# Two-layer attention in a vision tower: projection in f16 passes, transfers issued by ScalarE, a new order of transfers, doubled values

## What is computed

```python
def _L0_attn_ref(x, w_qkv, b_qkv, w_proj, b_proj):     # x: (64, 196, 192), normalized
    qkv = x @ w_qkv.T + b_qkv
    ...
    atten = jnp.einsum('bhqd,bhkd->bhqk', q, k) * SCALE
    atten = jax.nn.softmax(atten, axis=-1)
    out = jnp.einsum('bhqk,bhkd->bhqd', atten, v)
    out = jnp.transpose(out, (0, 2, 1, 3)).reshape(B, P, D)
    return out @ w_proj.T + b_proj
```

## Time and profile before

| | |
|---|---|
| median of three runs | 3193.28 us (3190.69 to 3194.79) |
| the profiled execution | 3213.14 us, its span 3211.4 us |
| busy in the span | PE 2835.8, DVE 2311.4, ACT 1874.4, POOL 1399.9 us |
| mean granted TensorE clock | 0.964 |

### The profile page before, as it was taken

The page is one execution under the profiler, slowest core; times in us unless marked ns, Lnnn a source line. Parts: engine busy times, 40 slices in busy tenths (PEclk is TensorE's granted clock), DMA queues, the critical chain, the costliest instruction groups (busy, mean ns, idle before and its releaser), DMA issues. The chain is left out here.

```text
span 3211.4 us, 94765 instructions
## 1 busy us (share of the span) xinstructions
PE 2835.8 (88%) x31231; PEld 2149.3 (67%) x31231; DVE 2311.4 (72%) x5442; ACT 1874.4 (58%) x3668; POOL 1399.9 (44%) x1954
## 2 busy tenths in 40 slices
PE   4999379999999999999999968898984999999997
PEld 4888245555555555555555538888864888888887
DVE  4888367777777777777777736766655777777776
ACT  3888246666666666666666637666642444444443
POOL 2777323333333344444444221565554444444444
PEclk9999579999999999999999989999987999999999
DMA  5664245556565666666666544444433433444443
GB/s 138 170 189 112 58 107 135 147 146 151 146 152 146 149 157 159 163 159 160 161 160 165 146 102 132 135 134 126 133 103 92 65 64 65 66 68 67 65 65 48
DMA packets 514471, 393.84 MB, mean 123 GB/s; under 512 B 222432, under 2 KB 487682, under 8 KB 514178
## 3 DMA queue, kind: packets, MB, share of 16 engines
q1 hardware_dynamic: 472514, 338.78, 41.4%
q0 software_dynamic: 38496, 46.38, 8.2%
q10 hardware_dynamic: 3168, 4.82, 0.6%
HBM read 232.59 MB, written 155.42 MB: 121 GB/s over the span
## 5 line engine op out<-in xcount | busy, mean ns | idle before, releaser
L657 DVE TENSOR_REDUCE a_mx<-a_mxp 98x4 f32<-98x784 f32 x768 | 746.4, 972 | 318.2 <-PE a_mxp L806 316.2
L533 ACT ACTIVATE a_pt<-a_st 98x784 f32<-98x784 f32 x768 | 632.3, 823 | 207.4 <-PE a_st L792 206.7
L1563 POOL DMA_INDIRECT out_dram<-f_yo,f_idg x202 | 330.9, 1638 | 432.5 <-DVE f_yo L1904 396.1
L479 POOL TENSOR_TENSOR a_cn<-a_ctxs,a_rec 128x392 f32<-128x392 f32 x192 | 190.0, 1019 | 531.8 <-DMA a_rec<-a_recip 531.8
L1641 ACT ACTIVATE f_hf<-f_bank,f_b1c 128x256 f32<-128x256 f32 x606 | 254.3, 473 | 236.1 <-PE f_bank L878 236.1
L821 PE MATMUL a_pv<-a_pt,a_vp 98*32 98x196 f32 x6144 | 339.0, 338 | 0.8 <-ACT a_ctxs L564 0.5
L868 PE MATMUL a_pr<-a_pf,a_cn 128*98 128x192 f32 x1536 | 332.1, 346 | 7.5 <-POOL a_cn L479 4.3
L2066 PE MATMUL f_bank<-f_w2h,f_hh 128*128 x1212 | 299.7, 247 | 25.1 <-DVE f_hl L1888 24.3
L806 PE MATMUL a_mxp<-a_kst,a_qst 48*128 48x196 f16 x3072 | 262.2, 248 | 67.1 <-DMA a_kst<-a_qk 46.5
L2067 PE MATMUL f_bank<-f_w2h,f_hl 128*128 x1212 | 298.2, 246 | 0.0
L2068 PE MATMUL f_bank<-f_w2l,f_hh 128*128 x1212 | 298.2, 246 | 0.0
(11 more groups left out here) (304 smaller groups left out, 7684.1 us busy)
## 6 DMA issues: line engine op xcount, KB each, us to landing
a_rec<-a_recip SPq DMA_DIRECT2D x256, 147.0 KB, 3.6
t_rows<-in_x_dram SPq DMA_DIRECT2D x84, 392.0 KB, 5.9
a_qst<-a_qk SPq DMA_DIRECT2D x256, 110.2 KB, 3.3
a_kst<-a_qk SPq DMA_DIRECT2D x256, 110.2 KB, 3.0
f_xg<-f_listed SPq DMA_DIRECT2D x101, 264.0 KB
a_qk<-a_qkh SPq DMA_DIRECT2D x128, 196.0 KB, 2.7
a_qk<-a_qkl SPq DMA_DIRECT2D x128, 98.0 KB, 2.9
a_qk<-a_qkh SPq DMA_DIRECT2D x128, 98.0 KB, 2.4
```

Of the source, the lines that this page charges most:

```text
L533: act.activation(pt[k % PT][:].rearrange("p j a t -> p j (a t)"), st_ps[0:half_t, :, 0:unit_t], ACT.Exp, scale=sm_scale).then_inc(exp_s, 1)
L657: dve.tensor_reduce(mx[:, a, :, 2 * p:2 * p + 2].rearrange("p q j -> p j q"), mx_ps[0:half_t, :, 0:unit_t].rearrange("p j (q t) -> p j q t ...
L1563: pool.indirect_dma_start(out, bass.IndirectOffsetOnAxis(ap=idg[i % 3][:, t:t + 1], axis=0), yo[i % 3][:, t, :], None, compute_op=ALU.add) ...
```

## The change

- The context is multiplied on POOL in one operation over all 1176 columns (`cf`), then a masked f16 half (`ch`) is made and subtracted, which leaves an f16 operand `cn` with high halves in the first 16 rows of each head's 32 and low halves in the last 16. For this the values `vp` hold each head's columns twice (second ScalarE copy, 15 columns), with the ones in the last column; the heads' columns lie 12 elements apart; and one more transfer copies context row 15 to row 31 when the sums were gathered.
- `project` is seven f16 products for each token tile (weights in a high and a low half `ph`, `pl`, and one product for the bias), two tiles into one PSUM bank, at slots 4 and 6; `out_rows` adds two tiles at once.
- `place_maxima`, the residual load and (second layer) the store of `xx` are issued by ScalarE at slots 3, 9, 8 and 0.
- SyncE's order is new, `store_parts` comes in four parts of which only the last waits for the third block of rows, and the tables of slots are new.

```diff
-        OUTS, NORM, REC = 4, 5, 64
-
-        ROWS_AT, TURN_AT, VALUES_AT = (9, 11, 6), (3, 5), (1, 2)
-        PROJECT_AT = ((2, 2, 2), (4, 4, 4), (6, 6, 6), (9, 10, 10))
-        HIGH_PART_AT, VALUES_OUT_AT = (4, 6), (1, 2)
-        LOW_PART_AT, LOW_ROWS_AT, OUT_AT = (4, 7), (9, 11, 6), (3, 4, 7, 11)
+        OUTS, NORM, REC = 2, 5, 64
+
+        ROWS_AT, TURN_AT, VALUES_AT = (9, 11, 6), (2, 3), (0, 1)
+        PROJECT_AT = (4, 4, 6, 6)
+        HIGH_PART_AT, VALUES_OUT_AT = (3, 6), (1, 2)
+        LOW_PART_AT, LOW_ROWS_AT, OUT_AT = (3, 7), (10, 11, 6), (5, 10)
         MAXIMA_AT = (2, 8)
 
-        ROWS_FIRST, PART_FIRST, CONTEXT_FIRST, VALUES_FIRST = (1, 1, 0), (0, 1), (1, 1, 1, 1, 1, 1), (0, 0)
-        NEGATED_AT, RECIP_AT, STATS_AT, AGGREGATE_AT = 6, 4, (10, 0), 2
+        ROWS_FIRST, PART_FIRST, CONTEXT_FIRST, VALUES_FIRST = (1, 1, 1), (0, 0), (0, 1, 1, 0, 0, 1), (0, 0)
+        NEGATED_AT, RECIP_AT, STATS_AT, AGGREGATE_AT = 7, 5, (9, 1), 4
...
@@ SyncE, step
                 if "M" in kinds:
                     load_stacks(s + 1, (par + 1) % 2, 1, 0)
+                if "M" in kinds:
                     load_stacks(s + 1, (par + 1) % 2, 1, 1)
                 if "P" in kinds:
                     store_parts(s + 2, par, 0)
+                    store_parts(s + 2, par, 1)
+                if "P" in kinds:
+                    store_parts(s + 2, par, 2)
...
-                if kinds.get("L") == 1:
-                    u = s + 3
-                    wait(sp, xx_s, 4 * (u - UL + 1))
-                    sp.dma_start(of_units(r_rows, u, 1), xx[:]).then_inc(res_s, 16)
-                if "C" in kinds:
-                    place_maxima(s, par, 1)
...
+                if "O" in kinds:
+                    u, b = s - 1, (par + 1) % 2
+                    waits(sp,
+                          (inv_s, u),
+                          (ctx_s, GROUPS * (u + 1)))
+                    sp.dma_start(sums[:], ctxs[b][2 * hd - 1::32].rearrange("h g (q t) -> h (g q) t", q=4)).then_inc(sum_s, 16)
+                if "O" in kinds:
+                    u, b = s - 1, (par + 1) % 2
+                    waits(sp,
+                          (cn_s, 3 * u - 2),
+                          (sum_s, 16 * (u + 1)))
+                    sp.dma_start(ctxs[b][2 * hd - 1::32], ctxs[b][hd - 1::32]).then_inc(dup_s, 16)
...
+                if "P" in kinds:
+                    load_stacks(s + 2, par, 0, 0)
+                if "P" in kinds:
+                    store_parts(s + 2, par, 3)
...
-                if "M" in kinds:
-                    place_maxima(s + 1, (par + 1) % 2, 0)
...
@@ POOL, step
                     wait(pool, pr_s, OUTS * (u - 1))
+                    wait(pool, cn_s, 3 * u)
+                    wait(pool, dup_s, 16 * (u + 1))
                     wait(pool, rec_s, REC * (u + 1))
-                    for g in range(3):
-                        pool.tensor_tensor(cn[b][:, g, :], ctxs[b][:, g, :], rec[:, g, :], ALU.mult).then_inc(cn_s, 1)
-
+                    pool.tensor_tensor(cf[:], ctxs[b][:], rec[:], ALU.mult).then_inc(cn_s, 1)
+                    pool.wait_ge(cn_s, 3 * u + 1)
+                    pool.tensor_tensor(ch[:], cf[:], low_half[:].unsqueeze(2).to_broadcast([128, 3, unit_t]), ALU.mult).then_inc(cn_s, 1)
+                    pool.wait_ge(cn_s, 3 * u + 2)
+                    pool.tensor_tensor(cn[b][:], cf[:], ch[:], ALU.subtract).then_inc(cn_s, 1)
...
@@ ScalarE, step
                     empty(k, 0)
+                    if k == 0 and kinds.get("L") == 1:
+                        u = s + 3
+                        wait(act, xx_s, 4 * (u - UL + 1))
+                        act.dma_start(of_units(r_rows, u, 1), xx[:]).then_inc(res_s, 16)
+                    if k == 3 and "C" in kinds:
+                        place_maxima(s, par, 1)
+                    if k == 8 and "O" in kinds:
+                        u, b = s - 1, (par + 1) % 2
+                        waits(act,
+                              (xo_s, OUTS * (u - 1) + 1),
+                              *(((res_s, 16 * (u - UL + 1)),) if kinds["O"] == 1 else ()))
+                        act.dma_start(xres[b][:], of_units(r_rows, u, kinds["O"])).then_inc(xres_s, 16)
+                    if k == 9 and "M" in kinds:
+                        place_maxima(s + 1, (par + 1) % 2, 0)
...
-                order = "p (x h d) -> p x h d" if layers[layer][7] else "p (x d h) -> p x h d"
-                act.copy(vp[b][:, 2 * n:2 * n + 2, :, 0:hd],
-                         misc[BANK[f"V{n}"]][0:half_t, 0:2 * dim].rearrange(order, x=2, h=heads)).then_inc(vp_s, 1)
+                order = "p (x h d) -> p x d h" if layers[layer][7] else "p (x d h) -> p x d h"
+                rows = misc[BANK[f"V{n}"]][0:half_t, 0:2 * dim].rearrange(order, x=2, h=heads)
+                pair = slice(2 * n, 2 * n + 2)
+                act.copy(vp[b][:, pair, 0:dim].rearrange("p x (d h) -> p x d h", h=heads), rows)
+                act.copy(vp[b][:, pair, dim:2 * dim - heads].rearrange("p x (d h) -> p x d h", h=heads),
+                         rows[:, :, 0:hd - 1, :]).then_inc(twice_s, 1)
...
-                wait(act, cn_s, 3 * (u - 2) + g + 1)
+                wait(act, cn_s, 3 * (u - 2) + 1)
...
@@ TensorE
-                if g6 % 3 == 0:
-                    wait(pe, vp_s, 2 * u + a + 1)
+                if g6 == 0:
+                    wait(pe, twice_s, 2 * (u + 1))
...
-                        ins = pe.matmul(pv_ps[32 * h4:32 * h4 + 32, 0:tok], vp[b][:, 2 * a + kt, h, :], pt[(first + h4) // 2 % PT][:, h4 % 2, kt, :],
+                        ins = pe.matmul(pv_ps[32 * h4:32 * h4 + 32, 0:tok], vp[b][:, 2 * a + kt, :].rearrange("p (c h) -> p c h", h=heads)[:, :, h], pt[(first + h4) // 2 % PT][:, h4 % 2, kt, :],
...
-                if x == 0:
-                    wait(pe, cn_s, 3 * u + g + 1)
-                ins = pe.matmul(pr_ps[0:half_t, 0:dim], cn[b][:, g, x * half_t:(x + 1) * half_t], pf[layer][:, g, :],
-                                start=(g == 0), stop=(g == 2))
-                if g == 2:
+                    wait(pe, cn_s, 3 * (u + 1))
+                ts, at = slice(x * half_t, (x + 1) * half_t), x % 2 * dim
+                ins = products(pe, pr_ps[0:half_t, at:at + dim],
+                               [(ones16[:], pl[layer][:, 3, :])]
+                               + [(cn[b][:, g, ts], w[layer][:, g, :]) for g in range(3) for w in (ph, pl)])
+                if x % 2 == 1:
                     ins.then_inc(pr_s, 1)
```

More of the change, by code:

```diff
@@ L109, in attention_phase @@
         wl = [sb(f"wl{i}", [128, 2, 3 * dim], F16) for i in range(NL)]
-        pf = [sb(f"pf{i}", [128, 3, dim], F32) for i in range(NL)]
+        pbias = [sb(f"pbias{i}", [rows_q, 2, 128], F32) for i in range(NL)]
+        pf = [sb(f"pf{i}", [128, 4, dim], F32) for i in range(NL)]
+        ph = [sb(f"ph{i}", [128, 4, dim], F16) for i in range(NL)]
+        pl = [sb(f"pl{i}", [128, 4, dim], F16) for i in range(NL)]
         bq = [sb(f"bq{i}", [128, QB], F32) for i in range(NL)]
@@ L191, in attention_phase @@
         sum_s = sem("sum_s")
+        dup_s = sem("dup_s")
         inv_s = sem("inv_s")
@@ L420, in _ @@
             for layer in range(NL):
-                pool.memset(praw[layer][:], 0.0).then_inc(consts, 1)
+                pool.memset(pbias[layer][:], 0.0).then_inc(consts, 1)
             pool.memset(ident[:], 0.0).then_inc(consts, 1)
@@ L569, in maxima_row, with place_maxima @@
                 act.copy(mrow[:, a, :], pv_ps[0:heads, 0:tok]).then_inc(mr_s, 1)
+            def place_maxima(u, b, a):
+                waits(act,
+                      (mr_s, 2 * u + a + 1),
+                      (ms_s[a], 32 * u))
+                for j in range(2):
+                    at = 64 * j + STACK
+                    act.dma_start(qst[b][at:at + 1, :, a, 0:tok], mrow[j::2, a, :]).then_inc(ms_s[a], 16)
             steps(step, act, between)
@@ L600, in prepare @@
                 dve.wait_ge(p_ok[layer], done + 2)
-                dve.tensor_reduce(praw[layer][:, :, :, hd + 1:hd + 2], pbv[:], AX.X, ALU.add).then_inc(p_ok[layer], 1)
+                dve.tensor_copy(praw[layer][:, :, :, hd:2 * hd], praw[layer][:, :, :, 0:hd]).then_inc(p_ok[layer], 1)
+                for part in range(2):
+                    dve.tensor_reduce(pbias[layer][:, :, 32 * part:32 * part + 1], pbv[:].rearrange("p e h d -> p e (h d)"),
+                                      AX.X, ALU.add).then_inc(p_ok[layer], 1)
                 dve.wait_ge(w_f[layer], G_READY[layer])
@@ L774, in step @@
                         for x in range(4):
-                            for g in range(3):
-                                if PROJECT_AT[x][g] == k:
-                                    project(s - 2, par, x, g, kinds["Y"])
+                            if PROJECT_AT[x] == k:
+                                project(s - 2, par, x, kinds["Y"])
                     if k == MAXIMA_AT[0] and "C" in kinds:
```

122 lines of the change are left out of this document (60 added, 62 removed).

## The result

| | before | after | forecast |
|---|---|---|---|
| time, median (us) | 3194.03 (3190.69 to 3197.79) | 3167.61 (3162.98 to 3171.36) | 3097 (3045 to 3210) |
| ratio to before, 95% interval | 1 | 0.9915 (0.9897 to 0.9933) | 0.970 |
| profiled span (us) | 3211.4 | 3169.6 | |
| one step (us) | 22.77 | 22.33 | 21.2 |

The change makes the kernel faster by 0.85%, 27 us (3194 x 0.0085), inside the range, and gives little more than a quarter of the 96 us that were forecast. The step follows from the first and last reciprocal, as in the earlier trace rows: (1866.5 - 459.8) / 63 = 22.33 us, 0.44 less, x 64 = 28 us. The two spans lie 41.8 us apart, since the profiled execution of before was itself 20 us above its median and that of after 4 us; I go by the steps and the medians.

A forecast was written before the change was run, and what follows sets the result against it. TensorE's work plus late transfers was taken as the bound. TensorE 20.6, VectorE 19.4 and POOL's loop 20.4 to 21.3 us gave a 21.2 us step; 100 us gained less 4 gave 3097 us, range 3045 to 3210.

The forecast's parts named there:

- TensorE works 21.28 us a step: TensorE before the change: 21.28 us of work in a 22.77 us step, the other 1.5 us nearly all late transfers.
- anything that takes TensorE work out pays, until another loop closes: TensorE in each step: removing its work shortens the step; the f16 projection was to remove 2.2 us.
- the gain is not there: Rival, 4%: loops other than TensorE's already set the step, so the time is 3193 + 4 us.
- Projection 2.5 us: TensorE's projection: 28 f16 products at 0.082 us, plus 0.1 us behind each of two blocks, against 4.68 us today.
- TensorE's 19.1 us: TensorE's work per step after the change, 2.2 us lower through the f16 projection.
- The K stacks are issued 1.5 to 3 us earlier than today, so most of the 13.6 us of waits ... goes: SyncE's queue: earlier K-stack transfers save TensorE 0.8 us of waiting a step.
- The maxima for slot 6 ... stays or grows to 0.5 us: TensorE's wait for maxima placed by DMA: issued about when they were, while TensorE arrives sooner; up to 0.5 us.
- The negation on VectorE: VectorE's negated maxima no longer stand between maxima (0.97 us) and low half, taking 0.6 us off the POOL loop.
- stands ahead of the reciprocals' store, which waits for VectorE until slot 5 anyway, so it is covered: SyncE's wait for the sums costs nothing extra; without that cover, at most 5.13 us.
- ScalarE's issues overlap its work: ScalarE's queue: 3.5 to 4 us of new issues a step, each pair hidden under the preceding exponential and gap.
- ScalarE pays for its issues: Rival, 20%: two issue pairs at 0.7 us each in a loop TensorE waits for; step 22.2 to 22.4, 3167 us.
- POOL 8.0 to 8.9 us: POOL's three dependent passes over 1176 columns (multiply, masked f16 half, subtract) take 8.0 to 8.9 us together.

The follow-up runs named there:

- A: The changed kernel with ScalarE issuing the residual load in slot 11 instead of slot 8: 3212.29 us against 3198.58 for the kernel before, ratio 1.0057.
- B: The changed kernel without VectorE's negation of the maxima, ScalarE scaling the row as it copies it: 3159.20 us against 3198.58 for the kernel before, ratio 0.9872.
- the fast step: Step of the changed kernel with A, B and C together: 20.44 us, ratio 0.9568 to the kernel before.
- C: The changed kernel with SyncE issuing the sums' transfer ahead of the part-2 stores, output and input: 3162.14 us against 3202.04 for the kernel before, ratio 0.9884.

## Why the prediction was right in sign and wrong in size

- **"TensorE works 21.28 us a step", "anything that takes TensorE work out pays, until another loop closes": the step that failed.** The f16 projection alone gave 0.07 us of the 2.2. The other loop was already closed, and the earlier trace rows had a sign of it: TensorE ended a wait for a transfer nearly every step. I read these waits as a sum on top of its work; they were evidence that something else sets the pace. The rival that said so, *the gain is not there*, had 4%. Nor was 21.28 us all work: it is busy time, with short waits hidden in it, and the work is about 20.2 us by the estimate above.
- **Projection 2.5 us**: the terms were right. 14 products take 1.3 us against 1.25 (1199.65 to 1200.94 in after's timeline), and by the distances between starts TensorE's work fell by 2.0 us from before to after, against 2.2.
- **TensorE's 19.1 us in after: 20.26 busy.** 0.3 us is the granted clock, which the forecast took as unchanged, 0.25 us the strided loads' part in the weighted sums. The rest, some 0.6 us, is most likely waits too short to show as idle time: the work is some 18.2 us by the same estimate.
- **"The K stacks are issued 1.5 to 3 us earlier than today, so most of the 13.6 us of waits ... goes": right**, 34.6 us to none.
- **"The maxima for slot 6 ... stays or grows to 0.5 us": wrong in size and in place.** It is 0.86 us a step, at slot 0 in 47 of 49 steps, and the cause is in the change itself: the residual load, moved to ScalarE at slot 8, stands ahead of the maxima issued at slot 9. Moving it three slots took the wait from 42.3 to 0.4 us. I had priced that load by its issue alone (0.5 us), and not asked which transfers stand behind it on its new queue.
- **The negation on VectorE: priced at its busy time, and not looked at beside POOL.** I counted what it no longer delays, but the change also makes POOL's instructions 2.7 times as long (2.68 us against 2.96 / 3), and the negation waits for one out. With cut passes the same kernel goes from 0.9955 to 0.9598.
- **The wait for the sums "stands ahead of the reciprocals' store, which waits for VectorE until slot 5 anyway, so it is covered": wrong.** SyncE stands 2.5 us a step in it. The reciprocal itself waits for the sums, so the cover begins only when the wait ends. Issuing the sums earlier takes 0.45 us off after's step, and 0.81 off the kernel with A and B (21.25 to 20.44).
- **ScalarE's issues overlap its work: right**, by the timeline above. The rival *ScalarE pays for its issues* gave 3167 us, which is the time measured, but its mechanism is refuted: a number that fits is no evidence.
- **POOL 8.0 to 8.9 us: 7.3** (2.68 + 2.15 + 2.43). The loop through POOL, forecast as one of three equal limits, is none: TensorE waits 4.4 us in 49 steps for `a_cn`, and leaving two passes out changes the fast step by 0.01 us.
- **Strided loads, 0 to 28 ns, upper end 83: 41 ns**, above what I took and above the break-even of 33 ns, which was worked out for a load in full view. The loads are hidden; removing the stride gained nothing measurable twice.
- **Clock 0.99: wrong where it mattered.** It was listed among the signs of error but had no term. A stall costs its length and may cost as much again or more at 1.2 GHz (2.1 us and 3.4 on top in A), so that edits which each remove one of several stalls gain little or lose (A: +1.4 points), and the same edits together gain 3.5 points. Where the clock is at 1.00 the forecast step comes out: 21.25 us with A and B, though with stalls of another kind than the forecast's.

The forecast step of 21.2 us was in reach, then, though not by this change: with the three flaws mended it is 20.44, and the kernel takes 0.957 of the time before.

Not settled: what bounds the step of 20.44 us (TensorE's work is about 18.1 of it; the waits that are left name ScalarE's copies of values and exponentials), and why the clock falls behind one stall and not behind another of like length (with A and B a stall of 2.78 us at 1176 to 1179 is followed by 0.50, and one of 2.27 us that ends at 1594.26 is not: 1.00 from 1594.3 to 1602). Issuing the maxima from SyncE again was not tried.

## What to carry to other kernels

If a busy engine ends a short wait for the same transfer in nearly every step, don't take its work for the bound: first ask who issues that transfer and what stands ahead of it in that queue, and give a small, urgent transfer its place before a large one. Busy time can hold waits that are shorter than an instruction's record; the distance between starts shows them. Keep POOL's instructions short where VectorE has small operations on SBUF beside them. Test mends together as well as alone when stalls cost clock, since one that is left can hide the gain of the rest.

## What the runs showed of the hardware

- A 24-column `tensor_scalar` on VectorE takes 0.17 to 2.27 us, and where it is long it ends with the POOL instruction beside it (1214.90 and 1214.87; 1243.86 and 1243.82). Reductions of the same engine stay at 0.95 to 0.98 us, 0.96 beside a POOL pass.
- In the steps shown, TensorE stood still for 1.5 to 2.1 us and was granted a clock of 0.50 soon after, for 6 to 7 us (worked out from the means of the stretches, as (1 - 0.70) x 2 x 3 + 3 + (1 - 0.67) x 2 x 3 = 6.8 in kernel A): sixteen matmuls take 1.55 us for 0.91. Not every such stall has it. That costs 0.3 us a step more than before in after, and 2.05 in the kernel with A and C.
- Two placements of 2.3 KB whose issue by ScalarE begins 1.7 us behind that of a 294 KB load (median) are waited for until 4.95 us behind the second of them; without the load ahead they are there within 3.98 us.
- DMA issues of ScalarE (0.35 to 0.69 us) run beside its activations.
- A weight load of 32 f32 columns takes 110 ns side by side and 151 ns at a stride of 48 bytes.
